# Second attention of a two-layer gated block: scores by head pairs on 32 rows, and VectorE's steps regrouped

## What is computed

```python
scores = jnp.einsum('bhqd,bhkd->bhqk', qh, kh) / math.sqrt(hd)   # 16 heads, hd = 16
causal = ki <= qi
scores = jnp.where(causal[None, None], scores, -10000.0)
attn = jax.nn.softmax(scores, axis=-1)
out = jnp.einsum('bhqk,bhkd->bhqd', attn, vh)
x = x + jnp.tanh(g_xattn[1]) * attention(_layernorm(x), ctx, ctx)
```

## Time and profile before

| | us |
|---|---|
| runs | 718.68, 720.95, 723.33 |
| median | 720.95 |
| profiled execution | 717.33 |
| its span | 715.6 |

### The profile page before, as it was taken

One profiled execution on the slowest core, in us unless ns is written; L12 is line 12 of the kernel. 1 busy time (PEld: TensorE's weight loads), 2 busy tenths in 40 slices (PEclk: granted clock), 3 DMA queues, 4 the chain that ended last, 5 costly groups with the idle time before them and its releaser, 6 DMA issues. The chain is left out here.

```text
span 715.6 us, 11503 instructions
## 1 busy us (share of the span) xinstructions
PE 575.2 (80%) x3938; PEld 456.6 (64%) x3938; DVE 487.9 (68%) x859; ACT 333.2 (47%) x572; POOL 207.1 (29%) x223
## 2 busy tenths in 40 slices
PE   5798250389999999974378668879899999999996
PEld 2476130389999999962134366656677667767775
DVE  2387934287778787615679978764778878778764
ACT  2442030277686867730367535364354454454431
POOL 4232207200000000017468531511534533543300
PEclk9999665589999999995589979887999999999997
DMA  8410005675866768125021020200210211201001
GB/s 280 170 35 14 0 0 191 200 257 171 270 211 236 241 215 265 46 92 176 11 75 44 1 87 0 84 0 1 82 67 18 83 43 40 82 24 59 1 1 59
DMA packets 49037, 70.36 MB, mean 98 GB/s; under 512 B 6391, under 2 KB 40926, under 8 KB 47966
## 3 DMA queue, kind: packets, MB, share of 16 engines
q1 hardware_dynamic: 46734, 64.49, 27.5%
q0 software_dynamic: 1568, 4.20, 1.8%
q10 hardware_dynamic: 688, 1.05, 0.5%
HBM read 58.71 MB, written 11.03 MB: 97 GB/s over the span
## 5 line engine op out<-in xcount | busy, mean ns | idle before, releaser
L864 PE MATMUL bank<-xhi,wlo 128*128 128x256 f32 x240 | 68.4, 285 | 4.0 <-issue 4.0
L1484 POOL TENSOR_TENSOR wlo<-raw,whi 128x1408 fp32r<-128x1408 f32 (+1 forms) x16 | 46.1, 2901 | 77.4 <-ACT whi L1489 77.4
L864 PE MATMUL bank<-xhi,whi 128*128 128x256 f32 x240 | 68.2, 284 | 0.0
L864 PE MATMUL bank<-xlo,whi 128*128 128x256 f32 x240 | 68.0, 283 | 0.0
L882 PE MATMUL bank<-whi,hlo 128*128 128x256 f32 x240 | 67.7, 282 | 0.0
L882 PE MATMUL bank<-wlo,hhi 128*128 128x256 f32 x240 | 66.5, 277 | 0.0
L882 PE MATMUL bank<-whi,hhi 128*128 128x256 f32 x240 | 66.5, 277 | 0.0
L1953 PE MATMUL bank<-xhi,wlo 128*128 128x512 f32 x128 | 55.8, 436 | 2.4 <-DVE xlo L2055 2.4
L1141 POOL DMA_INDIRECT ceg<-moe_const,crow x1 | 0.9, 918 | 187.3 <-DMA moe_const<-yb 187.3
L1085 DVE TENSOR_TENSOR hlo<-ga,hhi 128x512 fp32r<-128x512 f32 x60 | 40.1, 689 | 19.9 <-ACT hhi L932 19.9
L929 ACT ACTIVATE ga<-bank,b1s 128x256 f32<-128x256 f32 x120 | 49.6, 465 | 5.1 <-PE bank L864 3.6
(11 more groups left out here) (325 smaller groups left out, 1621.1 us busy)
## 6 DMA issues: line engine op xcount, KB each, us to landing
raw<-w_in SPq DMA_DIRECT2D x16, 1024.0 KB, 5.0
rawb<-w_in SPq DMA_DIRECT2D x14, 1024.0 KB, 6.1
raw<-wf_in SPq DMA_DIRECT2D x8, 1088.0 KB
moe_rows<-zrow SPq DMA_DIRECT2D x1, 3840.0 KB, 14.5
xs<-moe_rows SPq DMA_DIRECT2D x15, 256.0 KB, 6.5
moe_out<-yb SPq DMA_DIRECT2D x15, 256.0 KB
scb<-sc_in SPq DMA_DIRECT2D x16, 160.0 KB
cv<-ctx_in SPq DMA_DIRECT2D x32, 64.0 KB, 2.2
```

Source lines behind the costliest of these rows:

```text
L864: last = nc.tensor.matmul(psum[b][:, half:half + ST], w[:, s, at:at + P], a[:, s, k, :], start=(n == 0), stop=(n == 3 * KT - 1))
L1484: nc.gpsimd.tensor_tensor(wlo[:, s, a:b], raw[:, a:b], whi[:, s, a:b].bitcast(F32), ALU.subtract).then_inc(to, 1)
```

## The change

`kx` of the second attention holds two masked copies of the keys (of the first and of the second head of each group of 32 rows), not eight; its mask is `pmask[:, 4:6]`, which the first layer uses already. A product takes 32 rows, 64 queries straight from `qT` and 128 columns; the four groups of 32 rows write four banks, in which both halves and both batches lie. All four banks belong to one tile at a time. `scores` is one piece, ahead of the transposes. `qs` and the ScalarE copies into it are gone. GpSimd's key loop is written out. TensorE's loop over tiles is unrolled. In `masked` VectorE does the four maxima (one for each bank), then both row maxima, then both subtractions. The mask term has four products of 256 columns, not two of 512.

```diff
@@ -112,6 +112,7 @@
         ident = buf("ident", [P, P])
         hmask = buf("hmask", [P, HT])
         tg = buf("tg", [P, 4])
+        pmask = buf("pmask", [P, 6])
         stats = buf("stats", [P, NT, 6])
         mv = buf("mv", [P, NT, 2])
         rstd = buf("rstd", [P, NT])
@@ -277,7 +278,6 @@
             zrow = buf1("zrow", [P, D])
 
             kx = buf1("kx", [P, XC, KT, 2, S])
-            pmask = buf1("pmask", [P, 6])
             kx_ready = sem("kx_ready")
             vx = buf1("vx", [P, XC, HP, 2 * VC])
             vx_zero = sem("vx_zero")
@@ -1115,7 +1115,7 @@
 
             far_r = buf("far_r", [P, S], F32R, s5)
             ident_r = buf("ident_r", [P, P], F32R, s5)
-            kx = buf("kx6", [P, XC, KT, HT, S], F32, s5)
+            kx = buf("kx6", [P, XC, KT, 2, S], F32, s5)
             kx_ready = sem("kx6_ready")
             n5 = Norm(hn, 3, 2)
             ws_loaded, ws_ready, wsh_ready = sem("ws_loaded"), sem("ws_ready"), sem("wsh_ready")
@@ -1149,7 +1149,7 @@
                     n5.power(pool)
                     pool.wait_ge(ld5, 16)
                     for j in range(2):
-                        split_keys(pool, ctxT, kx, kx_ready, j, j, hmask[:, :])
+                        split_keys(pool, ctxT, kx, kx_ready, j, j, pmask[:, 4:6])
 
                 @block.tensor
                 def _(pe):
@@ -1214,7 +1214,6 @@
 
             sems4.close()
             with ExitStack() as s6:
-                qs = buf("qs6", [P, XC, KT, S], F32, s6)
                 cv = buf("cv6", [P, XC, D], F32, s6)
                 vx = buf("vx6", [P, XC, HP, 2 * VC], F32, s6)
                 sm = buf("sm6", [P, XR, KT, HT, S], F32, s6)
@@ -1223,10 +1222,10 @@
                 rc = buf("rc6", [P, XR, NH], F32, s6)
                 o = buf("o6", [P, XR, NH, HD], F32, s6)
                 cv_in = [sem(f"cv6_in{j}") for j in range(XC)]
-                vx_zero, qs_ready, vx_ready = sem("vx6_zero"), sem("qs6_ready"), sem("vx6_ready")
+                vx_zero, mx_ready, vx_ready = sem("vx6_zero"), sem("mx6_ready"), sem("vx6_ready")
                 s_done, s_read, e_ready = sem("s6_done"), sem("s6_read"), sem("e6_ready")
                 p_turned, pt_ready, pv_done, o_added = sem("p6_turned"), sem("pt6_ready"), sem("pv6_done"), sem("o6_added")
-                mask_step, out_step = sem("mask_step"), sem("out_step")
+                sub_ready, out_step = sem("sub6_ready"), sem("out_step")
                 NI = B // XC
 
 
@@ -1244,12 +1243,13 @@
                     @block.gpsimd
                     def _(pool):
                         for j in range(2, XC):
-                            split_keys(pool, ctxT, kx, kx_ready, j, j, hmask[:, :])
-                        with pool.Fori(1, NI) as it:
-                            for j in range(XC):
-
-                                pool.wait_ge(s_done, XC * it + 2 * (j // 2) + 2)
-                                split_keys(pool, ctxT, kx, kx_ready, XC * it + j, j, hmask[:, :])
+                            split_keys(pool, ctxT, kx, kx_ready, j, j, pmask[:, 4:6])
+                        for n in range(NT):
+                            s = n % XR
+                            if n + XR < NT:
+                                pool.wait_ge(s_done, 2 * n + 2 + XC)
+                                for h in range(2):
+                                    split_keys(pool, ctxT, kx, kx_ready, 2 * (n + XR) + h, 2 * s + h, pmask[:, 4:6])
 
                         for h in range(NS):
                             pool.wait_ge(wsh_ready, h + 1)
@@ -1262,25 +1262,27 @@
                         pe.sem_inc(s_done, XC)
                         pe.sem_inc(pv_done, XC)
 
-                        def scores(tile, k):
+                        def scores(tile):
                             n, s = tile
-                            if k == 0:
-                                pe.wait_ge(kx_ready, KT * (2 * n + 2))
-                                pe.wait_ge(qs_ready, 2 * n + 2)
-                            pe.wait_ge(s_read, KT * n + k + 1)
-                            nc.tensor.matmul(psum[KT * s + k][:, :], ident_r[:, :], rows(far_r[:, :], HT),
-                                             start=True, stop=False)
-
-                            for h in range(2):
-                                last = nc.tensor.matmul(psum[KT * s + k][h * S:(h + 1) * S, :],
-                                                        qs[:, 2 * s + h, k, :],
-                                                        kx[:, 2 * s + h, k, :, :].rearrange("p h s -> p (h s)"),
-                                                        start=False, stop=True)
-                            last.then_inc(s_done, 1)
+                            pe.wait_ge(kx_ready, KT * (2 * n + 2))
+                            pe.wait_ge(s_read, NR * (n + 1))
+                            for r in range(NR):
+                                nc.tensor.matmul(psum[r][:, 0:2 * KT * S], ident_r[:, :], rows(far_r[:, :], 2 * KT),
+                                                 start=True, stop=False)
+                            for k in range(KT):
+                                for h in range(2):
+                                    own = slice(h * S, (h + 1) * S)
+                                    for r in range(NR):
+                                        dims = slice(32 * r, 32 * r + 32)
+                                        last = nc.tensor.matmul(psum[r][own, 2 * k * S:2 * (k + 1) * S],
+                                                                qT[dims, k, (2 * n + h) * S:(2 * n + h + 1) * S],
+                                                                kx[dims, 2 * s + h, k, :, :].rearrange(
+                                                                    "p h s -> p (h s)"), start=False, stop=(k == KT - 1))
+                            last.then_inc(s_done, 2)
 
                         def step(tile, nxt, _):
                             if nxt is not None:
-                                scores(nxt, 0)
+                                scores(nxt)
                             n, s = tile
                             for k in range(KT):
                                 pe.wait_ge(e_ready, KT * n + k + 1 + KT * XR)
@@ -1290,9 +1292,6 @@
                                                                sm[:, s, k, 2 * q:2 * q + 2, :].rearrange(
                                                                    "p h s -> p (h s)"), ident[:, :])
                                 last.then_inc(p_turned, 1)
-                            for k in range(1, KT):
-                                if nxt is not None:
-                                    scores(nxt, k)
                             pe.wait_ge(pt_ready, KT * (n + 1) + KT)
                             pe.wait_ge(o_added, n + 1)
                             pe.wait_ge(vx_ready, 2 * (2 * n + 2) + 2 * XC)
@@ -1305,13 +1304,12 @@
                                     if hp == HP - 1:
                                         last.then_inc(pv_done, 1)
 
-                        for k in range(KT):
-                            scores((0, 0), k)
-                        over_tiles(pe, step)
+                        scores((0, 0))
+                        over_tiles(pe, step, unrolled=True)
 
                     @block.vector
                     def _(dve):
-                        dve.sem_inc(s_read, KT * XR)
+                        dve.sem_inc(s_read, NR)
                         dve.sem_inc(o_added, XR)
                         v = Steps(dve, vx_zero)
                         v(nc.vector.memset(vx[:, :, :, :], 0.0))
@@ -1322,19 +1320,22 @@
                         def masked(tile):
 
                             n, s = tile
-                            v = Steps(dve, mask_step, n * 2 * KT)
                             dve.wait_ge(p_turned, KT * (n + 1))
+                            dve.wait_ge(s_done, 2 * n + 2 + XC)
+                            for r in range(NR):
+                                part = sm[:, s, :, 2 * r:2 * r + 2, :]
+                                nc.vector.tensor_tensor(
+                                    part, psum[r][:, 0:2 * KT * S].rearrange("p (k h s) -> p k h s", k=KT, h=2),
+                                    lo_b[:, :].unsqueeze(1).unsqueeze(1).broadcast_to([P, KT, 2, S]), ALU.max
+                                    ).then_inc(s_read, 1)
+                            dve.wait_ge(s_read, NR * (n + 2))
                             for k in range(KT):
-                                dve.wait_ge(s_done, 2 * n + k + 1 + XC)
-                                bank = psum[KT * s + k][:, :].rearrange("p (h s) -> p h s", s=S)
-                                part = sm[:, s, k, :, :]
-
-                                nc.vector.tensor_tensor(part, bank, rows(lo_b[:, :], HT), ALU.max
-                                                        ).then_inc(s_read, 1)
-                                dve.wait_ge(s_read, KT * n + k + 1 + KT * XR)
```

(24 more changed lines are left out.)

## The result

The changed kernel takes a median of 725.37 us (20 runs) against 723.38 us for the kernel before (20 runs beside them). The ratio is 1.0059, with a 95% interval of 1.0034 to 1.0084: 4.3 us slower (2.5 to 6.1). The medians stand only 2.0 apart because they take in a few executions in a second, slower state of the chip that any kernel can meet, and every ratio here compares the others alone. The difference is less than the 1% that the forecast calls a difference, but it lies on the other side of zero, and the time is above the stated range (711.0 to 722.5). The profiled execution is 727.34 us with a span of 725.6 us.

A forecast was written before the change was run, and what follows sets the result against it. A ring between TensorE and ScalarE, 5.86 us a tile, was taken to bound the second attention. Gains 2.1 + 1.4 + 1.4 - 0.8 = 4.1 us: median 716.9, say 717.0; range 711.0 to 722.5.

The forecast's parts named there:

- Part 1: Norm before the second attention: narrow keys cut GpSimd's instruction from 1.05 to 0.40 us; block ends 2.1 us sooner.
- Part 2: Start of the second attention: query copies go, worth nothing; a luckier load of `cv` could give up to 1.3.
- T(0): First transpose of tile 0 in the second attention; forecast to hang on the load, not on the query copies.
- Part 3: Steady tiles of the second attention: 5.50 us a tile instead of 5.86, 1.4 us won over four tiles.
- last guard: Against a slow clock in the steady tiles: TensorE's new busy share, 76%, compared with 74% that kept 1.00.
- rival (c): Row groups don't overlap at 64 columns, or clock 0.50 acts likewise: slower, about 729 us; chance 0.08.
- the ring: TensorE and ScalarE by turns in each tile: 1.92 + 1.18 + 1.70 + 0.70 = 5.50 us, before 5.86.
- VectorE: Masked tile takes 3.9 us, not 4.5; with output steps 5.1 to 5.2 a tile, under 5.50.
- Part 4: End of the second attention: low parts hit tile 5; 1.4 us won, less 0.8 for slow clock after TensorE's idle gap.
- rival (a): VectorE's second subtraction gets in ahead of GpSimd's second low part: 7.4 us won, 713.5 us; chance 0.17.
- T(6): First transpose of tile 6 in the second attention; forecast 13.6 us after that of tile 4.
- T(4): First transpose of tile 4 in the second attention; the forecast counts the times of the end from it.

The follow-up runs named there:

- wide_norm: Changed kernel plus the norm's four former 128x512 GpSimd products, into a buffer nothing reads; ratio 1.0048 to the kernel before.
- order_only: Kernel before with only the order changed: both halves of the next scores issued ahead of the transposes; ratio 1.0025.
- fill2_pieces: Changed kernel with the far (mask) term computed three times and GpSimd's low parts cut into 16 pieces; ratio 0.9926 to the kernel before.
- fill1_pieces: Changed kernel with the far (mask) term computed twice and GpSimd's low parts cut into pieces; ratio 0.9902 to the kernel before.
- fill2: Changed kernel with the far (mask) term computed three times, only the last counting; ratio 1.0017 to the kernel before.
- before_light: Kernel before with score products covering half the key columns, part of the computation left out; ratio 1.0050.
- ungrouped: fill2_pieces with VectorE reducing and subtracting tile half by tile half again; ratio 0.9905 to the kernel before.
- warm_pieces: fill2_pieces with six more discarded products just ahead of the first transposes; ratio 0.9936 to the kernel before.
- behind: fill2_pieces with the next scores issued behind the transposes, ahead of the value products; 743.85 us, ratio 1.0294 to the kernel before.

## Why the prediction was right or wrong

- **Part 1, right.** 2.1 us were forecast, 2.2 came, by the mechanism named: it goes with the width of GpSimd's instruction and returns with it (wide_norm). The four took 1.69 for a forecast of 1.6.
- **Part 2, about right.** The values of the first tile still wait for the load of `cv` (2.42, then three times some 0.5), as before. T(0) came 9.1 us after the attention's first preparation, before 9.9: 0.8 where nothing was counted and "up to 1.3" allowed. The 0.8 is no gain of the change: the kernels built from before have 8.5 to 9.4.
- **Part 3, the step that failed** is its last guard: "against that, a busy share of 74% kept 1.00 and the new one is about 4.2 / 5.5 = 76%". The clock did not stay: it was 0.50 from 363.1 to 417.7, and a tile took 7.01 us, not 5.50. The 76% rested on the score that Part 3 had overpriced, 2.0 us. It took 1.35 (wide_norm), so TensorE's work in a tile is 3.6, not 4.2, and the guard's own sum gives 3.6 / 5.5 = 65%; measured at 1.00 it is 3.59 of 5.46 us, 66%, and no longer near the 74%. The step should have listed what the change takes from TensorE: score products of 2 x 1.08 us a tile (their size in order_only) become one of 0.69. The prediction named the outcome in its rival (c) ("score near 3.5, products 1.9, ring 7.5"; measured 2.3, 1.95, 7.01), but gave the whole rival 0.08. A share taken where the clock is slow would not have warned: the changed kernel is busy 43.2 of 54 us, 80%, at 0.50, and fill2_pieces 29.8 of 37 us, 81%, at 1.00, since the slow clock itself stretches busy time.
- **Part 3, the ring itself, right but for the clock.** Where the clock is 1.00, 5.43 for 5.50. The price of the scores was too high: "I take 2.0" was 1.35, a far term of 0.73 and products of 0.69 (at 0.50: 1.23 and 1.16, together 2.3). The Trainium skill (TensorE: Matmul & The Clock Gate, The mechanism) has products in different positions run at once, and the prediction worked out 1.4 by it, for all eight positions; the measured 1.35, with 32 records in 0.69 us, agrees with it. That cheapness was counted as harmless, since it was hidden. Work added back in the same place restored the clock (fill1_pieces, fill2), so it was what cost it.
- **VectorE, right.** A masked tile is 1.42 + 1.28 + 1.28, about 3.9 from 386.31 to 390.23 in the changed kernel, as forecast, and no wait of the ring is for VectorE before the low parts. The regrouping gains nothing, since VectorE wasn't what the ring waited for.
- **Part 4, right in mechanism, wrong in weight.** The low parts met tile 5, and the second subtraction came after the second low part, as forecast against rival (a). In a ring at 1.00 this costs 4.0 us, in the one at 0.50 it costs 1.0. The forecast had T(6) 13.6 us after T(4), 2.6 more than two steps of 5.5; in fill2 it came 15.0 after. The Trainium skill (SBUF — State Buffer, Who interferes with whom) has VectorE's two-input instructions contend with GpSimd's reads, which fits 5.58 for two and 1.79 in pieces.
- **What stays open: what the clock goes by.** Less work for TensorE lost it (the change, before_light), more held it (fill1_pieces, and fill2 with the pieces or without). Taken in the steady part and at 1.00 alone, the busy shares go with that: 80% (before, 368 to 403), 81% (fill2_pieces) and 73% (fill1_pieces) kept it, 66% (wide_norm) and 54 to 58% (before_light) did not. But at its start the kernel before was busy only 3.09 of 6.00 us (362 to 368), and its clock stayed at 1.00. How it rises differs too: just ahead of the rise TensorE was busy without a pause in the kernel before, fill2 and fill1_pieces, while the changed kernel at 0.50 still idles 0.19 and 0.69 us in each tile; yet in wide_norm the clock rose in spite of such a pause. The runs show the direction of the effect, not the quantity that decides it.
- **What stays open: the rest of the time.** The blocks account for +1.1 of the measured +4.3 (changed kernel again: +1.3 of +4.1), and in fill2_pieces for -8.5 where the times say -5.3 (-7.6 to -3.2). In fill1_pieces (-7.3 for -7.1) and ungrouped (-6.9 for -6.9) they agree. One place differs besides: the first layer's attention, same code in all, takes 34.4 to 34.5 us in most profiles, but 38.4, 38.4 and 44.9 in three (the changed kernel again, fill2_pieces, fill2), where its clock was at 0.50 for part of it, and in none of the four profiles of kernels built from before. In fill2 its stretch is this, with a mean clock of 0.69 where the changed kernel's first profile has 1.00:

```profile
29.00:73.00 44.00, 40.24 (x560) 32.89 (x560) 25.67 (x80) 15.51 (x24) 8.99 (x24) 0.69 0.09 26
```

Three out of ten against none out of four can be chance. It comes and goes between runs of one kernel: the profiled run of fill2_pieces, which has it, took 718.30 us at a mean clock of 0.879, and six of its nine compared runs took 713.15 to 714.30 at 0.889 to 0.892. If it isn't chance, the change does something to a stage 300 us ahead of it, and nothing here shows how.

## What to carry to other kernels

Before TensorE work is made cheaper in a stage whose time is set by a ring through other engines, look at the granted clock of that stage and ask whether what is left still holds it. The work removed may have been hidden, and its removal can make dearer what is not hidden: here TensorE's two parts of the ring went from 3.02 us at 1.00 (fill2_pieces) to 4.61 at 0.50. Work out TensorE's busy share of a tile at 1.00, with what the cheaper work will really take, and compare it with stretches that kept the clock; a share read at 0.50 tells little. That is a first look and no rule (see above). Where little is left, discarded products put into a wait can pay: about 0.5 us of them per tile, an estimate from 1.21 - 0.73 (fill1_pieces, wide_norm), were enough here for 5.43 us instead of 7.01. In the path they cost most of what they take (1.8 of 2.42 us in warm_pieces).

Where instructions of VectorE and GpSimd take turns, GpSimd's are better short: in pieces they took 9.3 us, not 6.2, and nobody waited. Here that paid only where the clock held; in the changed kernel and in the one before, the time doesn't show it.

## What the runs showed of the hardware

- Less work can take longer. Halving the score products' columns in the kernel before and nothing else made most tiles 6.9 to 7.0 us, not 5.86.
- Between a stage that keeps the clock and one that loses it there is a third kind: in before_light and behind the clock changed level again and again to the end of the stage (means 0.77 and 0.73).
- 16 fp32 products (32 records) of 32 rows, 64 weight columns and 128 moving columns, over eight positions of the array, take 0.69 us at 1.00 and 1.16 at 0.50, weight loads 0.45 and 0.76.
- Two VectorE subtractions and two GpSimd subtractions of 1280 columns, both queued back to back, went strictly by turns: 5.58 us for VectorE's two, 1.28 alone, 1.79 against pieces of 160 columns.
